# Reordering the start-up of a peer-layer pipeline: Gelus grouped, one tile's search moved, an order of its own for the first turn

## The reference

```
x1 = attention(x)                         # all 16 tiles first, then a batch norm over all tokens
sim = batchnorm(x1 @ w_q) . keys          # 2 x 8 heads x 32 keys
sx, sy = top 8 of 32 keys on each side, per head
scores = top 8 of the 64 sums sx + sy     # per head; the 8th is the threshold
h = softmax(scores) * gelu(x1 . down_embed[indices])
x2 = x + sum over heads, experts: h * up_embed[indices]
gate = softmax(rmsnorm(x2) @ wg + ...);  cw = the two best of 8
c = sum_e cw_e * (relu(relu(x2n W1_e + b1) W2_e + b2) W3_e + b3)      # experts of layer 1
g = sigmoid(c @ Wg), the two best of 8
out = x2 + sum_e g_e * (gelu(c F1_e + b) F2_e + b')                    # experts of layer 2
```

## Time and profile before

| | us |
|---|---|
| median of 3 runs | 833.32 (830.81 to 833.34) |
| the profiled execution | 831.08 |
| its span | 829.30 |
| TensorE busy | 777.6 (94%) |
| ScalarE busy | 579.4 (70%) |
| VectorE busy | 547.5 (66%) |
| GpSimd busy | 316.6 (38%) |

### The profile page before, as it was taken

One profiled execution on the slowest core, in us unless ns is written; L12 is line 12 of the kernel. 1 busy time (PEld: TensorE's weight loads), 2 busy tenths in 40 slices (PEclk: granted clock), 3 DMA queues, 4 the chain that ended last, 5 costly groups with the idle time before them and its releaser, 6 DMA issues.

```text
span 829.3 us, 14537 instructions
## 1 busy us (share of the span) xinstructions
PE 777.6 (94%) x5194; PEld 688.5 (83%) x5194; DVE 547.5 (66%) x1450; ACT 579.4 (70%) x990; POOL 316.6 (38%) x231
## 2 busy tenths in 40 slices
PE   4999999897885799999999999999999999999998
PEld 2878878765884688989998898999899999899987
DVE  3566566445806897797697779769778875853522
ACT  2566666523986978896898789789778888753353
POOL 2122221114994936442472753446066362000000
PEclk9899999998897799999999999999999999999999
DMA  9930000000000000000000000000000000000000
GB/s 308 326 89 2 1 2 2 1 1 0 2 1 0 1 2 1 8 1 2 1 8 1 2 8 1 1 2 7 1 1 8 1 2 8 0 2 1 8 1 7
DMA packets 11015, 16.92 MB, mean 20 GB/s; under 512 B 664, under 2 KB 6976, under 8 KB 10688
## 3 DMA queue, kind: packets, MB, share of 16 engines
q1 hardware_dynamic: 10944, 15.99, 6.1%
HBM read 14.94 MB, written 1.05 MB: 19 GB/s over the span
## 4 chain that ended last, share of the span: by engine, by line
PE 83%; POOL 8%; issue 4%; DVE 3%; ACT 2%; DMA 1%; DVEq 0%; SPq 0%; ACTq 0%; POOLq 0%
PE banks L441 76%; POOL region L390 7%; PE banks L480 4%; PE banks L639 2%; ACT x1T_all L885 1%; ACT G_both L876 1%; DMA region<-in_pC 1%; DVE HF L1320 0%; PE banks L494 0%; PE banks L671 0%; DVE W_both L1314 0%; DVE W_both L1145 0%; PE banks L730 0%; DVE acc L1455 0%; PE banks L652 0%
## 5 line engine op out<-in xcount | busy, mean ns | idle before, releaser
L390 POOL TENSOR_TENSOR region<-sim 128x1024 f32<-128x1024 f32 x128 | 260.7, 2064 | 101.5 <-DVE top_keys L1271 63.6
L1003 ACT ACTIVATE HF<-banks,lpack 128x256 f32<-128x256 f32 x256 | 105.6, 480 | 55.4 <-PE banks L441 54.5
L938 ACT ACTIVATE region<-region,neg_thr 128x1024 f32<-128x1024 f32 x128 | 143.7, 1152 | 0.2 <-POOL region L390 0.2
L1314 DVE SCALAR_TENSOR_TENSOR W_both<-region,rz_rel,W_both 128x1024 f32<-128x1024 f32 x98 | 136.8, 1396 | 1.5
L441 PE MATMUL banks<-HF,w_sb 128*128 128x256 f32 x512 | 123.0, 384 | 8.6 <-DVE HF L1320 8.6
L441 PEld LDWEIGHTS banks<-f_sb,HF 128*128 128x128 f32 x1024 | 123.7, 192 | 3.4
L944 ACT ACTIVATE region<-region,dtop 128x1024 f32<-128x1024 f32 x114 | 125.6, 1145 | 0.6
L441 PE MATMUL banks<-f_sb,HF 128*128 128x128 f32 x1024 | 124.5, 275 | 0.0
L441 PE MATMUL banks<-cT,f_sb 128*128 128x256 f32 x512 | 122.7, 382 | 0.1
L441 PEld LDWEIGHTS banks<-HF,w_sb 128*128 128x128 f32 x512 | 94.6, 193 | 20.2 <-DVE HF L1320 9.0
L441 PEld LDWEIGHTS banks<-cT,f_sb 128*128 128x128 f32 x512 | 92.1, 190 | 16.3 <-issue 2.9
(11 more groups left out here) (157 smaller groups left out, 1032.4 us busy)
## 6 DMA issues: line engine op xcount, KB each, us to landing
w_sb<-in_w SPq DMA_DIRECT2D x1, 2048.0 KB, 14.0
...
```

The source lines that it names most:

```text
L390: pool.tensor_tensor(S[a][h].rearrange("p (i j) -> p i j", i=NK), sim[a][:, h, :].unsqueeze(2).broadcast_to([P, NK, NK]), sim[a][:, PH + h ...
L938: act.activation(S[a][h], S[a][h], ACT.Prelu, bias=neg_thr[t % 4][:, h:h + 1], alpha=STEEP).then_inc(h_L, 1)
L1003: m = act.activation(HF[e % 2][:, f, :], bank(2 + b, 256 * (f % 2), 256 * (f % 2) + 256), ACT.Gelu_apprx_tanh, bias=L("bf", 4 * e + f, 4 * ...
L1314: v.scalar_tensor_tensor(W[a], S[a][h], rz_rel[a][:, h:h + 1], W[a], ALU.mult, ALU.add).then_inc(h_w, 1)
```

## The change

All of it concerns the start of the peer layer and turn 1.

- **Gelus.** Those of tiles 0, 1 and 2 go to HF[0], HF[1] and G[0] and run one after another, ahead of the first load of the table with Exp. Tile 2's expert inputs are formed in banks 4 and 5, right behind tile 1's. The diagonals move to H2 (tile 0, now two instructions, one for each of two tensors) and G[1] (tile 1, so its weighted sums also wait for the third Gelu). The four matmuls with a zero matrix that opened banks 2 to 5 go; the first weighted matmul of a bank starts it.
- **Prelu a head ahead.** In the start and in turn 1 the Prelu of head n+1 stands ahead of the Exp of head n. The third head of tile 2 moves from the start into turn 1.
- **Tile 3's search.** `key_scores(3)` stands between the sixth and the seventh weighted head of tile 1, so that VectorE's search runs beside them; `top_sums(2)` goes behind `add_peer(1)`.
- **Turn 1.** `key_scores(4)` moves from slot 0 to slot 5. GpSimd's power of -1/2 goes ahead of tile 3's pair scores. ScalarE takes STEEPS_1 and EXPS_1, VectorE SUMS_1, and VectorE goes through its slots in the order 4, 5, 0, 6, 1, 7, 2, 8, 3, 9, ...

The diff, cut to its core, in the file's order: the tensors, then GpSimd, TensorE, ScalarE and VectorE:

```diff
+        act_of = [HF[n][:, :, :].rearrange("p a n -> p (a n)") for n in range(2)] + [G[n % 2] for n in range(2, B)]
+        dg = [[H2[h // 4][:, :, :].rearrange("p a (b n) -> p (a b) n", n=P)[:, h % 4, :] for h in range(PH)],
+              [G[1][:, P * h:P * h + P] for h in range(PH)]]
...
+                if g == 1:
+                    root()
                 if peer:
                     for h in range(7):
                         pair_scores(t + 1, 1, h)
...
             def expert_inputs(t, a, c):
-                if c == 0:
-                    wait(pe, t_G, t)
+                if c == 0 and t != 2:
+                    pe.wait_ge(t_G, t)
                     wait(pe, t_PT, t - 1)
+                b = 4 + c if t == 2 else c
...
             key_scores(0, 0)           
-            for k in range(4):
-                mm(bank(2 + k), square[:, :], weff[:, :], start=True, stop=False)
             expert_inputs(1, 1, 0)
             expert_inputs(1, 1, 1)
+            expert_inputs(2, 0, 0)
+            expert_inputs(2, 0, 1)
...
             peer_out(0, 0)
-            for h in range(2, 4):
-                weighted(1, h)
+            weighted(1, 2)
             x2_T(0, 0)
-            for h in range(4, 8):
+            for h in range(3, 6):
                 weighted(1, h)
             key_scores(3, 1)
-            expert_inputs(2, 0, 0)
-            expert_inputs(2, 0, 1)
+            for h in range(6, 8):
+                weighted(1, h)
             peer_out(1, 1)
...
-                    if s == 0 and more:
+                    if s == (0 if late else 5) and more:
                         key_scores(t + 2, 0)
...
             expert_inputs(1, 1)
+            expert_inputs(2, 0)
             load_table(ACT.Exp, 1)
             exp_top(0, 0)
+            steep_pairs(0, 0, 0)
+            for n in range(18):
+                if n < 17:
+                    steep_pairs((n + 1) // 8, (n + 1) // 8 % 2, (n + 1) % 8)
+                exp_pairs(n // 8, n // 8 % 2, n % 8)
+                if n == 2:
+                    exp_top(1, 1)
+                if n == 13:
+                    x2_T(0, 0, 0)
+                    squares(0, 0)
+                if n == 15:
+                    exp_top(2, 0)
...
+            STEEPS_1 = {0: [2], 1: [3], 4: [4, 5], 5: [6], 6: [7, 8], 7: [9, 10], 8: [11, 12], 9: [13, 14], 10: [15, 16],
+                        11: [17, 18], 13: [19], 14: [20], 15: [21, 22]}
+            EXPS_1 = {0: [2], 4: [3, 4], 5: [5], 6: [6, 7], 7: [8, 9], 8: [10, 11], 9: [12, 13], 10: [14, 15], 11: [16, 17, 18]}
...
+                parts = ([(H2[n][:, :, :].rearrange("p a (b n) -> p (a b) n", n=P), 4 * n, 4) for n in range(2)] if t == 0
+                         else [(G[1].rearrange("p (h n) -> p h n", n=P), 0, PH)])
+                for dst, h, n in parts:
...
-            top_sums(2, 0)
             key_sums(3, 1)
...
             add_peer(1, 1)
+            top_sums(2, 0)
...
+            SUMS_1 = {0: [1], 6: [2, 3], 7: [4], 8: [5], 9: [6, 7], 10: [9, 10], 11: [11, 12], 12: [13], 13: [14], 14: [15]}
...
+                slots = list(range(16)) if g != 1 else [4, 5, 0, 6, 1, 7, 2, 8, 3, 9, 10, 11, 12, 13, 14, 15]
+                for s in slots:
```

More of the change, by code:

```diff
@@ L192, in program @@
         H1 = [HF[0][:, 2 * n:2 * n + 2, :] for n in range(2)]
-        dg = [HF[1 - n][:, :, :].rearrange("p a (b n) -> p (a b) n", n=P) for n in range(2)]
         H2 = [sb(f"H2_{n}", [P, 2, 256]) for n in range(2)]
+        act_of = [HF[n][:, :, :].rearrange("p a n -> p (a n)") for n in range(2)] + [G[n % 2] for n in range(2, B)]
+        dg = [[H2[h // 4][:, :, :].rearrange("p a (b n) -> p (a b) n", n=P)[:, h % 4, :] for h in range(PH)],
+              [G[1][:, P * h:P * h + P] for h in range(PH)]]
         acc = sb("acc", [P, 2, P])
@@ L406, in turn, with root @@
                 t = 2 * g
+                def root():
+                    pool.wait_ge(g_msq, g)
+                    pool.tensor_tensor(rms[:, :], msq[:, :], mhalf[:, 0:2], ALU.pow).then_inc(g_rms, 1)
+                if g == 1:
+                    root()
                 if peer:
@@ L409, in turn @@
                         pair_scores(t + 1, 1, h)
-                if new:
-                    if g > 1:
-                        keep_x2(t - 1, 1)
-                    pool.wait_ge(g_msq, g)
-                    pool.tensor_tensor(rms[:, :], msq[:, :], mhalf[:, 0:2], ALU.pow).then_inc(g_rms, 1)
+                if new and g > 1:
+                    keep_x2(t - 1, 1)
+                    root()
                 if not peer:
@@ L743, in weighted @@
                 pe.wait_ge(t_dg, t + 1)
+                if t == 1:
+                    pe.wait_ge(t_G, 3)
                 pe.wait_ge(h_E, 8 * t + h + 1)
@@ L746, in weighted @@
                     m = mm(bank(2 + 2 * t + c // 4, P * (c % 4), P * (c % 4) + P), S[t][h][:, P * c:P * c + P],
-                           dg[t][:, h, :], start=False, stop=(h == 7 and c % 4 == 3))
+                           dg[t][h], start=(h == 0 and c % 4 == 0), stop=(h == 7 and c % 4 == 3))
                 m.then_inc(t_W, 1)
             key_scores(0, 0)
-            for k in range(4):
-                mm(bank(2 + k), square[:, :], weff[:, :], start=True, stop=False)
             expert_inputs(1, 1, 0)
             expert_inputs(1, 1, 1)
+            expert_inputs(2, 0, 0)
+            expert_inputs(2, 0, 1)
             key_scores(1, 1)
@@ L953, in expert_inputs @@
                 act.wait_ge(t_Hp, 2 * t + 2)
-                wait(act, t_PT, t - 1)
-                act.activation(G[a], banks[:, 0:2, :].rearrange("p c n -> p (c n)"),
+                if t > 2:
+                    act.wait_ge(t_PT, t - 1)
+                b = 4 if t == 2 else 0
+                act.activation(act_of[t], banks[:, b:b + 2, :].rearrange("p c n -> p (c n)"),
                                ACT.Gelu_apprx_tanh).then_inc(t_G, 1)
@@ L1046, in turn @@
                 late = new and g > 1
+                steeps, exps = (STEEPS, EXPS) if late else (STEEPS_1, EXPS_1)
                 def heads(s, at, do):
@@ L1066, in turn @@
                         exp_top(t + 2, 0)
-                        exp_pairs(t + 2, 0, 0)
+                        if late:
+                            exp_pairs(t + 2, 0, 0)
                     if s == 11 and new:
@@ L1070, in turn @@
                     if s < 12:
-                        heads(s, EXPS, exp_pairs)
-                        heads(s, STEEPS, steep_pairs)
+                        if late:
+                            heads(s, exps, exp_pairs)
+                            heads(s, steeps, steep_pairs)
+                        else:
+                            heads(s, steeps, steep_pairs)
+                            heads(s, exps, exp_pairs)
                     if s == 12 and new:
@@ L1410, in weigh @@
                 wait(v, t_x2p, t)
-                v.tensor_tensor(PT[:, :], banks[:, b:b + 2, :].rearrange("p c n -> p (c n)"), G[a],
+                v.tensor_tensor(PT[:, :], banks[:, b:b + 2, :].rearrange("p c n -> p (c n)"), act_of[t],
                                 ALU.mult).then_inc(t_PT, 1)
@@ L1495, in turn @@
                 late = new and g > 1
-                for s in range(16):
+                sums = SUMS if late else SUMS_1
+                slots = list(range(16)) if g != 1 else [4, 5, 0, 6, 1, 7, 2, 8, 3, 9, 10, 11, 12, 13, 14, 15]
+                for s in slots:
                     if s == 4 and new:
@@ L1552, in turn @@
                     if peer:
-                        for h in SUMS.get(s, []):
+                        for h in sums.get(s, []):
                             add_weights(t + h // 8, h // 8, h % 8)
```

27 lines of the change are left out of this document (4 added, 23 removed).

## The result

The changed kernel took 828.92 us in the median of 8 runs (826.33 to 829.66), the kernel before 833.3 (8 runs, 830.72 to 837.55): a ratio of 0.9932 with the interval 0.9906 to 0.9958, so 0.4 to 0.9% faster. I had forecast 831.0, a gain of 2.3 us; it is 4.4. The direction and the mechanisms held, and the gain was 2.1 us too small, as both of its parts were mis-sized.

The account below looks back on a forecast made before the run. How early TensorE starts its unbroken run bounds the kernel, with VectorE and ScalarE almost without slack before it. -5.4 to X plus +3.9 to the mark gave -1.5; -2.3 taken, so 831.0 us against 833.32, range 825 to 836.5.

Parts of the forecast that it names:

- Diagonals: Tile 0's second diagonal instruction on VectorE waits again for GpSimd's addition: dtop1 2.0 us later; 0 if it slips through.
- ScalarE's last exp of tile 1: End of ScalarE's start: cheaper heads and no wait for x2_T(0) outweigh later exp_top(1), 2.8 us earlier.
- K to X: Start, from tile 0's search to the end of tile 1's x2s (X): X 5.4 us earlier, 7.3 if the second diagonal slips through.
- the search took 4.55 ... so 0.9 to 1.8 more: weigh(1) 5.4 earlier: VectorE's search for tile 3: starts earlier but slowed by GpSimd's additions for tile 2; weigh(1) at 248.9 instead of 254.28.
- X to the mark: From tile 1's x2s to pair 0's second gate matmul on TensorE (the mark): 53.8 us against 49.9, +3.9.
- VectorE's column: VectorE's rows added up from X, with waits for GpSimd: weigh(2) at X+46.3; alone it would give the mark at X+52.6.
- ScalarE's end: ScalarE ends last in turn 1: Gelu table in at X+53.2, cT at 53.6, the mark at X+53.8.
- Waits: TensorE's 8.6 us wait for hidden1's Relu becomes waits for hidden1(4) and hidden1(5), some 8 us; groups behind run at lower clock.
- Sum: Start and turn 1 together: -1.5 us, or -3.4 with the diagonals slipping through; -2.3 taken between them.
- Rival 1: Turn 1 packs well: second diagonal slips through, VectorE meets GpSimd less; -6 to -9, 824.5 to 827.5 us; chance 0.22.
- Rival 2: Turn 1's tail: TensorE's last six groups also run at 1.2 GHz; +4.2, 837.5 us; chance 0.16.
- Rival 3: Nothing moves: turn 1 at +5.2 and diagonals' 2.0 give -0.2, 833.1 us; chance inside the forecast's 0.62.

Follow-up runs that it names:

- e1: The changed kernel with tile 0's diagonals written by one instruction of 1024 columns instead of two of 512; 826.01 us.
- e3: The changed kernel with each Prelu in the start right ahead of its own head's Exp, as before the change; 828.74 us.
- e4: The changed kernel with key_scores(3) behind all eight weighted heads of tile 1, two heads later; 831.38 us.
- e7: The changed kernel's start with turn 1 of the kernel before, tile 0's diagonals in one instruction and top_sums(2) ahead of add_peer(1); 822.14 us.
- e9: As e7, with some of VectorE's turn 1 sums later, sums 9 and 10 behind weigh(2); 821.45 us.
- e8: As e7, with mean square, logits and first Relus first in turn 1, GpSimd's root ahead of tile 3's additions, key_scores(4) late; 824.95 us.
- e10: The changed kernel with one diagonal instruction, top_sums(2) ahead of add_peer(1), an Exp and Prelu ahead of ScalarE's last Relu, sums 9, 10 behind weigh(2); 824.51 us.

## Why the prediction was right, and where its sizes were off

**Diagonals: right.** I took +2.0 on dtop1 against 0; it is +1.77, and e1 takes it back. The rule of the Trainium skill (SBUF — State Buffer, "SBUF: two separate sides") is that whoever starts first blocks the other fully. The trace agrees for the second half (4.67 for the two); dtop's 0.21 right behind a 0.51 row shows again that a short instruction can follow in.

**ScalarE's last exp of tile 1: nearly right.** I said 2.8 earlier, it is 3.4. A head costs 2.08 as worked out; e3 puts the Prelu ahead at 1.85 on this exp, where I had 1.8, and at 1.5 on X, and the wait for x2_T(0) is gone as said.

**K to X: right mechanism, mis-sized.** The step that failed in size is "the search took 4.55 ... so 0.9 to 1.8 more: weigh(1) 5.4 earlier". In after weigh(1) comes 7.07 earlier, measured from K. The two terms behind that: key_scores(3) reached VectorE 7.6 earlier and not 6.8 (done at 249.7 before, "done near 242.9" in the forecast), and the search lost 0.57 to GpSimd and not 0.9 to 1.8 (its pair sums took 0.93, not 2.40). e4 shows the first term alone: with key_scores(3) two heads later, 3.4 us of the gain are gone. Peer_out(1) did run at the lower level, 3.68, as taken.

**X to the mark: right mechanism, +2.8 in place of +3.9.** VectorE's column held at its end: weigh(2) was said at X+46.3 and stands at X+46.4 (301.74), and from cw on its ends are within 0.5 us. Ahead of that hidden1(1) and (2) were done at X+4.7 and X+7.9 and not at 6.8 and 9.3, but the wait for the gate's Exp, said to last until 9.7 and over at 9.5, took this up. ScalarE's did not: I had its table at X+53.2, it is in at X+52.1 (307.45). Its waits ahead of the Relus were 7.8 us (2.0, 3.6, 2.3) where I had added 8.8. So the step that failed in size here is ScalarE's end: the mark came where I had put VectorE alone, X+52.6. Which engine ends last is nearly a tie: TensorE's transpose of layer 1's sum waits for VectorE until 306.82, and cT starts 0.3 behind its end. The 1.28 of the load with cT's table in use 0.01 later (306.17, 307.46) shows no drain; the Trainium skill (ScalarE: Activation LUTs, "What ACT_TABLE_LOAD costs") has 2.66 with one, and the trace does not agree.

**Waits: right.** The 8.6 us wait did turn into waits for the Relus of hidden1(4) and (5), 4.36 and 2.05 and with the third 7.5 in all (said: some 8), and the groups behind them ran at the lower level. That it "looks like a gift" and isn't was the main point, and the runs show it twice: e7 and e9 keep the wait and are the fastest; e8 starts the layer early, then waits 12.3 at once, and loses 1.9 from X to the mark.

**Sum.** -5.4 + 3.9 = -1.5, and 0.8 more for the chance that the second diagonal slips through, gave -2.3; the runs give -7.2 + 2.8 = -4.4. The second diagonal did not slip through, so the 0.8 that brought the forecast nearer were luck: the two sums as worked out are 2.9 off. The mis-sized terms all erred against the change: 0.8 for key_scores(3), 0.8 for the search, 1.1 for ScalarE's end. The range of 825 to 836.5, 11.5 us wide, holds the 828.92.

**Rivals.** Rival 1 (turn one packs well, -6 to -9) needed X to the mark within 1 of before and the second diagonal slipping through; neither came. Rival 2 (low clock in the tail) needed a granted clock under 0.8 between X+37 and X+47; the stretch 291.8 to 304 has 0.98. Rival 3 (nothing moves) is out: its +5.2 was +2.8.

What the change is worth, piece by piece: key_scores(3) earlier 3.4, Prelu ahead 1.5, the wait for x2_T(0) and the rest of the start some 4, less 1.7 for the split diagonals; turn one's new orders take 2.8 back. Of these the first two and the split are measured alone. The 4 is what remains, and no run takes the wait for x2_T(0) by itself. The version that the experiments point to keeps the start and drops the new turn one; e7 and e9 run it, at 822.14 and 821.45 us. From K to the mark they are 5.4 and 6.3 us ahead of the changed kernel, and 4.6 and 4.7 of that are the edits' if the clock of peer_out(1) is taken out. What stays open is why the old turn still beats the new one by 0.85 once both are mended. The rows show only where it is lost: TensorE reaches peer_out of tile 2 at X+46.65 in e10 and at X+45.92 in e9.
